# Attention over eight tokens: two head pairs at a time instead of one, with the value products in front of the scores

## The chip, the cores and the metric

One core of a Trainium2 chip runs the whole program. The metric is the device time of one execution in microseconds (us). "TensorE" is PE in the rows (its weight loads are PEld), VectorE is DVE, ScalarE is ACT, GpSimd is POOL, SyncE is SP.

## The reference

Two layers stand behind each other; the change touches only the second. Cut to what matters of it:

```python
xn = _layernorm(x)                                    # x: 8 x 512 x 256
qkv = xn @ W_in.T + b_in                              # read as (s=8, b=512), 16 heads of 64
q = q * 64 ** -0.5
attn = einsum('bhsd,bhtd->bhst', q, k) + einsum('bhsd,std->bhst', q, k_dist)
attn = softmax(attn)                                  # over t = 8 keys
out = einsum('bhst,bhtd->bhsd', attn, v) + einsum('bhst,std->bhsd', attn, v_dist)
s = out @ W_out.T + b_out
g = silu(sqrt((xn @ cos(theta + theta_noise)) ** 2 + (xn @ sin(phi + phi_noise)) ** 2))
x = x + s * g
```

Each of the 512 sequences has only 8 tokens, so a head's scores are 512 little matrices of 8 by 8.

## The kernel before

Layer 1 runs over 8 groups of 512 tokens (64 sequences); the group's number is `i`. Blocks of 32 tokens (4 sequences) are multiplied with themselves, which gives 32 by 32 scores, and `apart` pushes those of other sequences to minus infinity. Every engine has its own program text, and semaphores join them; the order is written out by hand. For TensorE and ScalarE, `layer1_steps` gives it, as a list of steps (kind, k):

- `V`: values of a tile of 128 tokens, half the heads; `Q`, `K`: queries and keys of head pair k (128 rows, 512 tokens); `F`: the gate's two products. Each is six products of 512 columns into one of two PSUM banks `pr`, used in turn; ScalarE reads the bank. `three` (L1598) issues them.
- `S`: the scores of pair k into `s_ps` (L1687), small products on part of the array, into disjoint parts of the banks. The program has 32 of them per pair, and each runs as two, so the profile counts 64.
- `AV`: the value products of pair k into `o_ps` (L1703), again 64 in the profile.
- After the steps, `outputs(t, pairs)` (L1716) multiplies each pair's outputs with `W_out`, three products of 256 columns for each of four tiles t and eight pairs. Tiles 1 and 2 come first, into the `pr` banks. Between them stand the transposes of the next group's tokens (`transposes`, L1607), of the weights summed by distance (L1736), and last the products for these (L1745).

Between S and AV a pair goes through all the other engines: VectorE adds the distance scores (`scores`, L1885) and takes the maximum (L1888), GpSimd subtracts it (L2048), ScalarE takes the exponential (L1771), VectorE sums the keys (`key_sums`, L1896 to L1906), GpSimd multiplies with the reciprocal (`weigh`, L2055), and VectorE transposes (`transposed_blocks`, L1915) into `pt`, which AV reads. ScalarE copies the AV result (L1810, `ot_h`), and VectorE makes its low part (`low_outputs`, L1923), after which `o_ps` is free. `by_distance` (L1943) is 16 instructions of VectorE per group that sum the weights by distance. The intermediates `sc`, `ex`, `pt` have two buffers each, so a pair may follow while the last one is under way.

At the end of a group ScalarE makes the gate (L1815 square root, L1817 tanh, each with a table load) and then reads the next group's transposed tokens (L1760, L1761); VectorE makes their low part (L1851). The transposes share the bank `misc` (`misc_free`), so the one at L1736 must wait until L1851 has read the one before.

Of the kernel before, what the change touches and what calls it, by code (L numbers as in the profile page):

```python
# [19 lines left out]
ALU = mybir.AluOpType  # L20
# [33 lines left out]
HP = H1 // 2  # L54
OT_EARLY = 5
# [102 lines left out]
class Shared:  # L158
# [3 lines left out]
    def __init__(self, nc, ctx):  # L162
# [36 lines left out]
        self.pt = [low[:, i * TOK // 2:(i + 1) * TOK // 2].rearrange("p (h t k) -> p h t k", h=2, t=TT) for i in range(2)]  # L199
# [1213 lines left out]


# [5 lines left out]
def layer1(nc, io, shared, x1_dram, out):  # L1420
    with ExitStack() as ctx:
# [29 lines left out]
        sc, ex = sb("sc", [P, 2, 2, TT, BLK]), sb("ex", [P, 2, 2, TT, BLK])  # L1451
        mx, sm, rc = sb("mx", [P, 2, 2, TT]), sb("sm", [P, 2, 2, TT]), sb("rc", [P, 2, 2, TT])
        ec = sb("ec", [P, 2, 2, TT, NREL])
# [133 lines left out]
        def _(pe):  # L1587
# [55 lines left out]
            def body(i):  # L1643
# [7 lines left out]

                for kind, k in steps:
# [27 lines left out]
                    if kind == "S":  # L1680
                        pe.wait_ge(m.qk_ok, 2 * HP * i + 2 * k + 2)
                        wait(pe, m.sc_ok, HP * i + k)
                        stand_alone(pe, m.pe_passed)
                        for blk in range(NBLK):
                            q, t = blk % 4, blk // 4
                            for h in range(2):
                                mm = pe.matmul(s_ps[BLK * q:BLK * (q + 1), h, BLK * t:BLK * (t + 1)],  # L1687
                                               qt[D1 * h:D1 * (h + 1), k % 2, BLK * blk:BLK * (blk + 1)],
                                               kt[D1 * h:D1 * (h + 1), k % 2, BLK * blk:BLK * (blk + 1)],
                                               start=True, stop=True)  # L1690
                        mm.then_inc(m.s_psum, 1)
                    if kind == "AV":
                        pe.wait_ge(m.pt_ok, HP * i + k + 1)
                        if k == 0:
                            pe.wait_ge(m.v_ok, 2 * TT * (i + 1))
                            wait(pe, m.so_ok, TT * i)
                        wait(pe, m.ot_low, HP * i + k)
                        for blk in range(NBLK):
                            q, t = blk % 4, blk // 4
                            rows = slice(BLK * q, BLK * (q + 1))  # L1700
                            for h in range(2):
                                c = D1 * (2 * k + h)
                                mm = pe.matmul(o_ps[D1 * h:D1 * (h + 1), q, BLK * t:BLK * (t + 1)],  # L1703
                                               v[rows, t, c:c + D1], pt[k % 2][rows, h, t, :], start=True, stop=True)
                        mm.then_inc(m.o_psum, 1)

                def w_bank(t):
                    return (fin, pr[:, through_pr.index(("W", 1)) % 2, :], pr[:, through_pr.index(("W", 2)) % 2, :],
                            o_ps[:, 0, :])[t]

                def outputs(t, pairs):
                    for hp in pairs:
                        tokens = slice(t * P, (t + 1) * P)
# [456 lines left out]
```

## Time and profile before

| | |
|---|---|
| three timed runs | 1199.99, 1203.26, 1204.4 us; median 1203.26 |
| span of the profiled execution | 1204.5 us |
| TensorE, VectorE, ScalarE, GpSimd busy, share of the span | 96%, 75%, 56%, 47% |
| granted TensorE clock, mean over the span | 0.975 |
| layer 1 | about the last 564 us of the span |

The page says how long each engine was busy. A TensorE record lasts longer than the time until the next one starts, because products are pipelined; what a product costs is read from start to start. "Issue" behind an idle time means that the engine waited for nothing that the profile shows.

### The profile page before, as it was taken

The numbers are of one execution on the slowest core, as the hardware profiler recorded it, in microseconds if no ns is written. First come the engines' busy times: TensorE is split into PE (matmuls) and PEld (weight loads), VectorE is DVE, ScalarE is ACT, GpSimd is POOL, SyncE is SP. The second block draws the span as 40 slices with busy tenths as digits, with TensorE's granted clock in tenths as the row PEclk, the third lists the DMA queues.
The fourth block names the chain that finished last, engine by engine and source line by source line (L and its number), as shares of the span: only waits on it lengthen the run. The fifth ranks groups of instructions, "written<-read, shape, count | busy, mean of one in ns | idle before, by whom it ended". The sixth has DMA issues, their size and how long they took to land. (4 is left out here: it accounts for less than half of the span.)

```text
span 1204.5 us, 34940 instructions
## 1 busy us (share of the span) xinstructions
PE 1161.7 (96%) x14327; PEld 755.9 (63%) x14327; DVE 901.2 (75%) x1993; ACT 677.8 (56%) x1302; POOL 571.2 (47%) x599
## 2 busy tenths in 40 slices
PE   6999999999999999999989999999999999999997
PEld 5433444444444444443368787878879787887976
DVE  6777887868788887878275967778687767768766
ACT  4357676776777677666643544445344444535453
POOL 2156686776868586777622413232231413223131
PEclk8589999999999999999989999999999999999999
DMA  8445254553525345352240010010101001010100
GB/s 236 105 96 135 70 138 119 116 151 79 143 71 136 104 115 132 93 156 72 71 127 1 4 54 3 12 46 4 54 4 54 4 16 41 4 54 4 36 4 19
DMA packets 57998, 86.80 MB, mean 72 GB/s; under 512 B 8304, under 2 KB 38256, under 8 KB 57840
## 3 DMA queue, kind: packets, MB, share of 16 engines
q1 hardware_dynamic: 57680, 84.31, 26.6%
q8 instruction: 113, 1.85, 0.6%
q14 instruction: 45, 0.37, 0.1%
q10 hardware_dynamic: 160, 0.26, 0.1%
HBM read 50.40 MB, written 33.55 MB: 70 GB/s over the span
## 5 line engine op out<-in xcount | busy, mean ns | idle before, releaser
L1111 DVE TENSOR_REDUCE negmax<-s_bank 128x1 f32<-128x512 f32 x512 | 330.2, 679 | 74.3 <-PE s_bank L759 73.7
L1306 POOL TENSOR_TENSOR room<-room 128x512 f32<-128x512 f32 x248 | 310.9, 1286 | 121.7 <-ACT room L925 121.7
L925 ACT ACTIVATE room<-t_bank 128x512 f32<-128x512 f32 x512 | 284.1, 600 | 84.2 <-PE t_bank L769 80.6
L769 PE MATMUL t_bank<-qst,kst 50*128 50x512 f32 x512 | 202.6, 472 | 6.1 <-ACT room L925 5.7
L759 PE MATMUL s_bank<-kst,qst 48*128 48x512 f32 x512 | 195.6, 475 | 5.1 <-DVE negmax L1111 2.9
L769 PEld LDWEIGHTS t_bank<-qst,kst 50*128 50x128 f32 x512 | 82.1, 189 | 102.1 <-ACT room L925 62.2
L2068 POOL TENSOR_TENSOR win<-rt,apart 128x512 f32<-128x512 f32 x32 | 41.9, 1331 | 211.6 <-DVE rt L1874 211.6
L1598 PE MATMUL pr<-xt_h,win_h 128*128 128x512 f32 x256 | 105.9, 414 | 0.0
L2055 POOL TENSOR_TENSOR ex<-ex,rc 128x256 f32<-128x256 f32 x64 | 41.7, 652 | 130.1 <-DVE rc L1902 130.1
L1598 PE MATMUL pr<-xt_l,win_h 128*128 128x512 f32 x256 | 100.5, 393 | 0.0
L1598 PE MATMUL pr<-xt_h,win_l 128*128 128x512 f32 x256 | 100.5, 393 | 0.0
L759 PEld LDWEIGHTS s_bank<-kst,qst 48*128 48x128 f32 x512 | 80.7, 195 | 18.4 <-DVE negmax L1111 13.6
L1786 ACT ACTIVATE win<-pr 128x512 f32<-128x512 f32 x64 | 38.4, 601 | 84.2 <-PE pr L1598 84.2
L1794 ACT ACTIVATE qt<-pr,bqkv 128x512 f32<-128x512 f32 x64 | 44.1, 689 | 69.0 <-PE pr L1598 69.0
L1874 DVE SCALAR_TENSOR_TENSOR rt<-r,own,rt 128x256 f32<-128x256 f32 x112 | 69.0, 616 | 4.0
L784 PE MATMUL a_bank<-room,v_even 128*32 128x512 f32 x512 | 69.9, 619 | 0.2
L1943 DVE SCALAR_TENSOR_TENSOR p<-pc,own,p 128x256 f32<-128x256 f32 x128 | 67.1, 524 | 2.8
L784 PE MATMUL a_bank<-room,v 128*32 128x512 f32 x512 | 68.7, 609 | 0.3
L808 PE MATMUL d_bank<-room,pick 128*32 128x512 f32 x496 | 66.2, 606 | 0.0
L1810 ACT ACTIVATE ot_h<-o_ps 128x512 fp32r<-128x512 f32 x64 | 38.3, 599 | 48.0 <-PE o_ps L1703 48.0
L1794 ACT ACTIVATE room<-pr,bqkv 128x512 f32<-128x512 f32 x64 | 44.0, 687 | 29.3 <-PE pr L1598 29.3
L1703 PE MATMUL o_ps<-room,win 32*64 32x32 f32 x4096 | 56.6, 224 | 3.5 <-issue 3.2
(333 smaller groups left out, 2576.2 us busy)
## 6 DMA issues: line engine op xcount, KB each, us to landing
park<-qk_h SPq DMA_DIRECT2D x126, 128.0 KB, 2.4
qst<-park SPq DMA_DIRECT2D x64, 192.0 KB, 3.2
kst<-park SPq DMA_DIRECT2D x64, 192.0 KB, 4.2
park<-qk_l SPq DMA_DIRECT2D x64, 128.0 KB, 2.4
room<-in_x SPq DMA_DIRECT2D x8, 512.0 KB, 5.3
xr<-in_x SPq DMA_DIRECT2D x8, 512.0 KB, 6.0
room<-x SPq DMA_DIRECT2D x8, 512.0 KB, 4.0
out<-so SPq DMA_DIRECT2D x32, 128.0 KB, 1.7
```

The lines of the kernel that those rows point to most:

```text
L759: pe.matmul(s_bank[n % S_BANKS][:, :], qst[slot][rows, j, c * P:(c + 1) * P], kst[slot][rows, j, :], start=True, stop=True).then_inc(m.s_d ...
L769: pe.matmul(t_bank[w % 2][:, :], kst[slot][rows, j, c * P:(c + 1) * P], qst[slot][rows, j, :], start=True, stop=True).then_inc(m.t_done, 1)
L784: mm = pe.matmul(a_bank[BLK * h:BLK * h + BLK, :], v[b % 2][:, c, hg * P + h * DH0:hg * P + (h + 1) * DH0], probs[:, c, h, :], start=(c == ...
L808: mm = pe.matmul(d_bank[BLK * h:BLK * h + BLK, :], pick[:, hf, :], sums[:, pair, h, :], start=first, stop=last)
L925: act.activation(probs[:, c, j, :], t_bank[w % 2][:, :], ACT.Exp, scale=SCALE0).then_inc(m.exp_done, 1)
L1111: dve.tensor_reduce(negmax[:, i_par, 2 * odd + j, c:c + 1], s_bank[n % S_BANKS][:, :], X, ALU.max, negate=True).then_inc(m.max_done, 1)
L1306: add = pool.tensor_tensor(sums[:, pair, h, :], probs[:, 2 * pair, h, :], probs[:, 2 * pair + 1, h, :], ALU.add)
L1598: mm = pe.matmul(dst, a(kc), b(kc), start=(n == 0), stop=(n == 3 * KC - 1))
L1703: mm = pe.matmul(o_ps[D1 * h:D1 * (h + 1), q, BLK * t:BLK * (t + 1)], v[rows, t, c:c + D1], pt[k % 2][rows, h, t, :], start=True, stop=True)
L1794: act.activation((qt, kt)[side][:, k % 2, :], bank, ACT.Identity, bias=bqkv[:, HP * side + k:HP * side + k + 1]).then_inc(m.qk_ok, 1)
L1874: dve.scalar_tensor_tensor(dst, src, own[:, s:s + 1], dst, op0=ALU.mult, op1=ALU.add).then_inc(m.r_sum, 1)
L1943: dve.scalar_tensor_tensor(dst, pc[:, heads, :, :], own[:, s:s + 1], dst, op0=ALU.mult, op1=ALU.add).then_inc(m.p15_sum, 1)
```

## The change

Scores, softmax and value products are done for two head pairs (`PG = 2`, `NG = 4` sets) in one go. A step `S` or `AV` now issues twice as many small products; `sc`, `ex`, `pt`, `mx`, `sm`, `rc`, `ec` hold one set of twice the size and have one buffer instead of two; the instructions on VectorE, GpSimd and ScalarE for a set are one each, of twice the width. `AV` of a set stands directly in front of `S` of the set two later. The last two value steps stand behind all F steps, and between and behind them the output products of tiles 1 and 2 are split by pairs. The semaphore counts follow.

```diff
 def layer1_steps():
-    steps = [("V", k) for k in range(2 * TT)] + [("Q", 0), ("K", 0)]
-    for hp in range(HP):
-        if hp + 1 < HP:
-            steps += [("Q", hp + 1), ("K", hp + 1)]
-        else:
-            steps += [("F", 0)]
-        steps += [("S", hp)]
-        if hp >= 2:
-            steps += [("AV", hp - 2)]
-    return steps + [("F", 1), ("F", 2), ("AV", HP - 2), ("F", 3), ("AV", HP - 1)]
+    def queries_and_keys(g):
+        return [(kind, hp) for hp in range(PG * g, PG * (g + 1)) for kind in "QK"]
+
+    steps = [("V", k) for k in range(2 * TT - 2)] + queries_and_keys(0) + [("V", 2 * TT - 2), ("V", 2 * TT - 1), ("S", 0)]
+    steps += queries_and_keys(1) + [("F", 0), ("S", 1)]
+    for g in range(2, NG):
+        steps += queries_and_keys(g) + [("AV", g - 2), ("S", g)]
+    return steps + [("F", 1), ("F", 2), ("F", 3), ("AV", NG - 2), ("AV", NG - 1)]
+
+EXP_BEFORE = {("Q", 3): 0, ("Q", 5): 1, ("Q", 7): 2, ("F", 3): 3}
...
+                    if (kind, k) == ("AV", NG - 1):
+                        pe.wait_ge(m.wout_low, 1)
+                        pe.wait_ge(m.ot_low, HP * i + PG * (NG - 2))
+                        for t in (1, 2):
+                            free_pr(i, "W", t)
+                            outputs(t, range(PG * (NG - 2)))
                     if kind == "AV":
-                        pe.wait_ge(m.pt_ok, HP * i + k + 1)
+                        pe.wait_ge(m.pt_ok, NG * i + k + 1)
...
-                        wait(pe, m.ot_low, HP * i + k)
+                        wait(pe, m.ot_low, HP * i + PG * k)
...
-                first_pairs, last_pair = range(HP - 1), (HP - 1,)
-                pe.wait_ge(m.wout_low, 1)
-                pe.wait_ge(m.ot_low, HP * i + HP - 1)
-                for t in (1, 2):
-                    free_pr(i, "W", t)
-                    outputs(t, first_pairs)
+                for n, pairs in ((HP - PG, range(PG * (NG - 2), HP - PG)), (HP - 1, (HP - 2,))):
+                    pe.wait_ge(m.ot_low, HP * i + n)
+                    for t in (1, 2):
+                        outputs(t, pairs)
                 pe.wait_ge(m.ot_low, HP * (i + 1))
-                outputs(1, last_pair)
+                outputs(1, (HP - 1,))
                 if not last:
                     transposes(i + 1, 0)
-                outputs(2, last_pair)
+                outputs(2, (HP - 1,))
...
@@ (VectorE, transposed_blocks)
-                wait(dve, m.o_psum, n - 1)
+                wait(dve, m.o_psum, n)
...
@@ (VectorE, the group's body from its second pair set on)
+                for g in range(2, NG):
+                    scores(i, g)
+                    for j in range(PG):
+                        low_outputs(i, PG * (g - 2) + j)
+                    key_sums(i, g)
+                    by_distance(i, 0, range(4 * (g - 2), 4 * (g - 2) + 2))
+                    transposed_blocks(i, g)
+                    if g < NG - 1:
+                        by_distance(i, 0, range(4 * (g - 2) + 2, 4 * (g - 1)))
+                for j in range(PG):
+                    low_outputs(i, HP - 2 * PG + j)
+                by_distance(i, 0, range(NREL - 2, NREL))
+                by_distance(i, 1, range(2))
+                for j in range(PG):
+                    low_outputs(i, HP - PG + j)
+                by_distance(i, 1, range(2, NREL))
```

On TensorE, in the middle of a group, the program before has this at a value step (`s_ps` are scores, `o_ps` value products, `pr` the last rows of K and the first of the next Q):

```order
L1598 MATMUL pr<-xt_h,win_l_66 128x512
L1687 MATMUL s_ps<-room,qt 32x32 x32
L1703 MATMUL o_ps<-room,win 64x32 x32
L1598 MATMUL pr<-xt_h,win_h_63 128x512
L1598 MATMUL pr<-xt_l,win_h_63 128x512
```

It comes six times in a group, with 12 products of 512 columns between two of them. Now the same place reads

```order
L1596 MATMUL pr<-xt_h,win_l_66 128x512
L1722 MATMUL o_ps<-room,win 64x32 x64
L1698 MATMUL s_ps<-room,qt 32x32 x64
```

It comes twice in a group, with 24 products of 512 columns ahead of it: 128 small products of the program stand in one run where 64 stood. The other value and score steps stand alone now, 64 in a run.

On VectorE, from the last transpose of weights to the group's end, the program before has (`p` is `by_distance`, `ot_l` the low part of a pair's outputs, `xt_l` that of the next group's tokens)

```order
L1915 STREAM_TRANSPOSE room<-ex 128x256
L1923 TENSOR_TENSOR ot_l_late<-o_ps,ot_h_49 128x512
L1943 SCALAR_TENSOR_TENSOR p<-pc,own,p 128x32x8 x3
L1923 TENSOR_TENSOR ot_l_late<-o_ps,ot_h_49 128x512
L1943 SCALAR_TENSOR_TENSOR p<-pc,own,p 128x32x8 x5
L1950 COPY pd<-p 128x16x4
L1951 TENSOR_TENSOR pd<-p 128x16x4x7
L1851 TENSOR_TENSOR xt_l<-o_ps,xt_h 128x512
```

and now

```order
L1917 STREAM_TRANSPOSE room<-ex 128x512
L1925 TENSOR_TENSOR ot_l_50<-o_ps,ot_h_49 128x512
L1925 TENSOR_TENSOR ot_l_late<-o_ps,ot_h_49 128x512
L1945 SCALAR_TENSOR_TENSOR p<-pc,own,p 128x32x8 x4
L1925 TENSOR_TENSOR ot_l_late<-o_ps,ot_h_49 128x512 x2
L1945 SCALAR_TENSOR_TENSOR p<-pc,own,p 128x32x8 x6
L1952 COPY pd<-p 128x16x4
L1953 TENSOR_TENSOR pd<-p 128x16x4x7
```

Two low parts (pairs 4 and 5) and ten sums by distance stand behind the last transpose now, where one low part and eight sums stood between the last transpose and the last low part's end.

## Rows read from the trace of the kernel before

**Rows 1.** The page: busy time of two engines; the queue of instruction blocks
```profile
PE 1161.7 (96%) x14327; PEld 755.9 (63%) x14327; DVE 901.2 (75%) x1993; ACT 677.8 (56%) x1302; POOL 571.2 (47%) x599
...
q8 instruction: 113, 1.85, 0.6%
```

**Rows 2.** Windows: two groups of layer 1 (window, us, busy us of each engine, clock)
```profile
920.16:989.70 69.54, 69.12 (x1326) 58.12 (x1325) 52.68 (x127) 33.13 (x53) 20.32 (x27) 1.00 0.08 25
989.70:1060.83 71.13, 69.30 (x1325) 58.20 (x1325) 52.73 (x127) 32.99 (x53) 20.30 (x27) 1.00 0.08 25
```

**Rows 3.** Waits of TensorE's products, 640 to 1204 us (us, times, longest)
```profile
PE o_ps L1703 <- issue: 3.2, 5, 0.9
PE pr L1598 <- issue: 1.2, 1, 1.2
PE s_ps L1687 <- issue: 0.6, 2, 0.4
PE o_ps L1703 <- DVE ot_l_late L1923: 0.2, 1, 0.2
```

**Rows 4.** Timeline of TensorE, 881 to 884 us (start, length, engine, line, tiles)
```profile
881.27 0.39 PE L1598 MATMUL pr<-xt_l,win_h 128*128 128x512 f32 x1
881.50 0.40 PE L1598 MATMUL pr<-xt_h,win_l 128*128 128x512 f32 x1
881.82 0.76 PE L1687 MATMUL s_ps<-room,qt 64*32 64x32 f32 x64
882.51 0.86 PE L1703 MATMUL o_ps<-room,win 32*64 32x32 f32 x64
883.30 0.50 PE L1598 MATMUL pr<-xt_h,win_h 128*128 128x512 f32 x1
883.64 0.39 PE L1598 MATMUL pr<-xt_l,win_h 128*128 128x512 f32 x1
```

**Rows 5.** Timeline of TensorE, 1031 to 1038 us
```profile
1031.44 0.76 PE L1687 MATMUL s_ps<-room,qt 64*32 64x32 f32 x64
1032.13 0.86 PE L1703 MATMUL o_ps<-room,win 32*64 32x32 f32 x64
1034.17 0.50 PE L1598 MATMUL pr<-cs_h,xt_h 128*128 128x512 f32 x1 [1.18 <-issue]
...
1035.77 0.76 PE L1687 MATMUL s_ps<-room,qt 64*32 64x32 f32 x64
1036.45 0.79 PE L1703 MATMUL o_ps<-room,win 32*64 32x32 f32 x57
1037.89 0.31 PE L1703 MATMUL o_ps<-room,win 32*64 32x32 f32 x7 [0.65 <-issue]
```

**Rows 6.** DMA, 1030 to 1040 us: what was moved in 40 slices of 0.25 us
```profile
GB/s 0 0 0 0 0 0 0 66 0 0 0 0 0 0 0 0 0 0 0 0 0 0 66 0 0 0 0 0 0 0 0 0 0 0 33 0 0 0 0 0
```

**Rows 7.** Timeline of TensorE, 895 to 896 us
```profile
895.44 0.66 PE L1703 MATMUL o_ps<-room,win 32*64 32x32 f32 x40
```

**Rows 8.** Groups by form, 860 to 930 us (count, busy us, mean ns, idle before)
```profile
L1943 DVE SCALAR_TENSOR_TENSOR p<-pc,own,p 128x256 f32<-128x256 f32 x16 | 8.2, 514 | 0.4
```

**Rows 9.** Timeline of ScalarE, 903 to 911 us
```profile
903.69 0.60 ACT L1810 ACTIVATE ot_h<-o_ps 128x512 fp32r<-128x512 f32 x1 [0.29 <-PE o_ps L1703]
...
907.98 1.06 ACT L1817 ACTIVATE room<-room 128x1024 f32<-128x1024 f32 x1
909.71 0.60 ACT L1760 ACTIVATE room<-o_ps 128x512 f32<-128x512 f32 x1 [0.67 <-PE o_ps L1607]
910.20 0.59 ACT L1761 ACTIVATE xt_h<-o_ps 128x512 fp32r<-128x512 f32 x1
```

**Rows 10.** Timeline of TensorE, 909 to 913 us
```profile
909.08 0.60 PE L1607 MATMUL o_ps<-ident,room 128*128 128x128 f32 x4
...
912.75 0.60 PE L1736 MATMUL o_ps<-ident,pd 128*128 128x128 f32 x4
```

**Rows 11.** Timeline of VectorE, 902 to 911 us
```profile
910.83 0.69 DVE L1851 TENSOR_TENSOR xt_l<-o_ps,xt_h 128x512 fp32r<-128x512 f32 x1 [2.47 <-ACT xt_h L1761]
```

More of the change, by code:

```diff
@@ L1650, in body, with w_bank, outputs @@
                 pe.wait_ge(m.xt_low, KC * (i + 1))
+                def w_bank(t):
+                    return (fin, pr[:, through_pr.index(("W", 1)) % 2, :], pr[:, through_pr.index(("W", 2)) % 2, :],
+                            o_ps[:, 0, :])[t]
+                def outputs(t, pairs):
+                    for hp in pairs:
+                        tokens = slice(t * P, (t + 1) * P)
+                        for n, (x, w) in enumerate(((ot_h[:, hp, tokens], wout_h), (ot_h[:, hp, tokens], wout_l),
+                                                    (ot_l(hp)[:, tokens], wout_h))):
+                            pe.matmul(w_bank(t)[:, 0:E], x, w[:, hp, :], start=(hp == 0 and n == 0), stop=False)
                 for kind, k in steps:
@@ L1705, in body @@
-                        mm.then_inc(m.o_psum, 1)
[L1707 to L1713, printed above, removed]
-                        for n, (x, w) in enumerate(((ot_h[:, hp, tokens], wout_h), (ot_h[:, hp, tokens], wout_l),
-                                                    (ot_l(hp)[:, tokens], wout_h))):
-                            pe.matmul(w_bank(t)[:, 0:E], x, w[:, hp, :], start=(hp == 0 and n == 0), stop=False)
@@ L1718, in body @@
-                first_pairs, last_pair = range(HP - 1), (HP - 1,)
-                pe.wait_ge(m.wout_low, 1)
-                pe.wait_ge(m.ot_low, HP * i + HP - 1)
-                for t in (1, 2):
-                    free_pr(i, "W", t)
-                    outputs(t, first_pairs)
+                        wait(pe, m.ot_low, HP * i + PG * k)
+                        for j in range(PG):
+                            for blk in range(NBLK):
+                                q, t = blk % 4, blk // 4
+                                rows = slice(BLK * q, BLK * (q + 1))
+                                at = TT * BLK * j + BLK * t
+                                for h in range(2):
+                                    c = D1 * (2 * (PG * k + j) + h)
+                                    mm = pe.matmul(o_ps[D1 * h:D1 * (h + 1), q, at:at + BLK],
+                                                   v[rows, t, c:c + D1], pt[rows, 2 * j + h, t, :], start=True, stop=True)
@@ L2075, in body @@
                 pool.memset(p15[:, :, :, :], 0.0).then_inc(m.p15_zero, 1)
-                for k in range(HP):
-                    if k >= 1:
-                        weigh(i, k - 1)
-                    less_maximum(i, k)
-                    if k == 2 and not last:
-                        rstd_of(i + 1)
-                for t in range(TT):
-                    if t == TT // 2:
-                        weigh(i, HP - 1)
-                    pool.wait_ge(m.sq_ok, TT * i + t + 1)
-                    if t == 0:
-                        wait(pool, m.x2_ok, TT * i)
-                    pool.tensor_tensor(q2[:, t, :], sq[:, t % 2, 0:E], sq[:, t % 2, E:2 * E], ALU.add).then_inc(m.q2_ok, 1)
+                less_maximum(i, 0)
+                weigh(i, 0)
+                squares_sum(i, 0)
+                less_maximum(i, 1)
+                if not last:
+                    rstd_of(i + 1)
+                weigh(i, 1)
+                less_maximum(i, 2)
+                weigh(i, 2)
+                less_maximum(i, 3)
+                squares_sum(i, 1)
+                squares_sum(i, 2)
+                weigh(i, 3)
+                squares_sum(i, 3)
             over_batches(body)
```

173 lines of the change are left out of this document (81 added, 92 removed).

## The prediction, made before the changed kernel had run

> **What bounds the kernel now.** I read the page first. TensorE is busy 96% of the span, VectorE 75% [rows 1], so what counts is what TensorE issues and where it stops. Then the windows: a group of layer 1 takes 69.5 us, another 71.1 us, at the full clock, with the same products and nearly the same busy time of every engine [rows 2]. The reader is to see that 1.6 us went without any engine working more. Third, the waits of TensorE's products in layer 1: VectorE held them up for 0.2 us in all 564 us, nobody else did, but 5.0 us in eight waits is "issue" [rows 3]. So no data is late anywhere, and VectorE's load is not the bound: whatever the change takes from it lies beside TensorE's work and is costed at nothing.
>
> Fourth, the timeline, from start to start. A product of 512 columns takes 0.23 us. The last one in front of small products takes 0.32 (881.50 to 881.82), the first one behind them 0.34 (883.30 to 883.64). 64 score products take 0.69 us, 64 value products 0.79 [rows 4]. Fifth, the "issue" waits. Scores of one pair and its value products, from 1031.44 on, should be over after 0.69 + 0.79 = 1.48 us; the next product starts only at 1034.17, 2.73 us after them. The next such stop comes after 6 + 64 + 57 = 127 products, at 1037.89 [rows 5]. A product is two instructions, the weight load and the product, so the first stretch holds 128 times 2 = 256 instructions, and the second 254 and a few waits. The page has a queue "instruction" with 113 transfers and 1.85 MB, 16 KB each, for 2 times 14327 = 28654 instructions and some waits: about 256 in a block [rows 1]. In the slices one such block is moved at 1031.75 to 1032.0 and the next at 1035.5 to 1035.75 [rows 6]: each starts after TensorE has entered a block and is needed at that block's end. So TensorE stops wherever it runs through 256 instructions faster than the next block comes. With large products 256 instructions last many us; only small ones are fast enough.
>
> **The change, part by part.** (1) Fewer passages and longer runs. A group had ten runs of small products (S0, S1, six of S and AV, AV6, AV7) and has six. A passage in and out costs 0.32 + 0.34 - 2 x 0.23 = 0.20 us, so four fewer give 0.8 us. Within a run, the small products that come later are the cheaper ones: 40 of them make a record of 0.66 us [rows 7], 64 one of 0.86 [rows 4], so 24 cost 0.20 us, 8.3 ns each, where the step's mean is 11 or 12. 64 more in a step then cost 0.53 instead of 0.69 or 0.79. Two pairs cost 0.69 + 0.79 + 2 x 0.53 = 2.54 us against 2.96, four times in a group 1.7 us. Together 2.5 us in each of 8 groups: -20 us. No row shows a step of 128. Bounds: if the second 64 cost as much as the first, only the passages are left, -6 us; at the 7.6 ns between the records of 40 and of 57 (0.66 and 0.79 us) [rows 5, 7] it is -22. I take -20, because the second half of a step already runs as the additional products would.
>
> (2) Whole blocks of small products. A run of 512 instructions (AV and S, 128 products of the program, 256 in the profile) always holds at least one whole block of 256, wherever the blocks' limits fall. There are two such runs in a group, 16 in all. The work of such a block is 128 x 8.3 ns = 1.1 us and some 0.1 at the step's change, 1.2. What a block takes at least, when it begins with small products, is 2.73 us in one row and 3.72 in the other [rows 5], so 1.5 to 2.5 us are lost each time. The 2.73 belongs to a block that begins right behind large products, where the sequencer has run ahead and asks early; the new blocks mostly begin in the middle of small ones. I take 2.2: 16 x 2.2 = +35 us, bounds +24 and +40. Of the stops of before, 5.0 us of idle time and about 0.2 more each that the length of the records hides, 7 us, I let 6 go [rows 3]: runs of 256 instructions remain, but a stop in them needs the block's limit close to the run's start.
>
> The Trainium skill has this in "Runtime: NRT & Kernel Launch", section "Instruction fetch mechanics": an engine's instructions come in blocks of 16 KiB, 256 of them, the next asked for while one runs. The trace agrees, with 16 KB in each of 113 transfers. The same section gives TensorE room for 2048 instructions and says that the fetch is mostly hidden; by that a run of 512 would cost nothing, and the sum would end below before. A box beside it speaks of two lines of 16 KiB only, and by that the stops come; the stop at 1034.17 speaks for the box.
>
> (3) The group's end. ScalarE copies the last values, makes the gate and then reads the next tokens' transposes; VectorE takes their low part; only then is the bank free for the transposes at L1736. Before, ScalarE's copy starts at 903.69 and ends at 904.29, the gate behind it lasts until 909.04, 4.75 us, and the two reads end at 910.79 [rows 9], VectorE at 911.52 [rows 11], and TensorE wants the bank at 912.75 [rows 10]: 1.2 us to spare. TensorE fills the time from 903.6 with 72 products of 256 columns and a transpose; 45 of them up to 909.08 make 0.122 us each. Now 24 of the 72 stand ahead of the last value step. Behind it are 48: 5.9 us, 0.4 for the transposes and 0.2 for passages, 6.4. ScalarE has two copies there, 1.1 us (the spacing of its reads is 0.5), then 4.75 + 1.08, and VectorE 0.7: 7.7 us with a hand-over. TensorE waits 1.3 us in seven groups, +9. Ahead of it the last value step must wait until VectorE has taken the low parts of pairs 4 and 5, which stand behind the last weights' transpose and the sums by distance at 0.51 us each [rows 8]; I reckon 0 to 0.8 us late, 0.25 taken, +2. The wait for pair 6's low part, behind four more such sums (2.1 us), mostly lies inside the 1.3. Together +11, bounds +6 and +18. Queued behind these waits on TensorE is all the rest of the group, so they count in full.
>
> Sum: -20 + 35 - 6 + 11 = +20 us, on the profiled 1204.5: 1224.5. The median of the runs shown is 1.2 lower, so 1223 for the timed run. The step from large to small products has no other wait in it: the drain of K by ScalarE (0.7 us) lies under the 1.3 us of value products in front of the scores. Without that cover it would cost about 0.7 us twice a group, 11 us.
>
> **The rivals.** (a) The blocks cost nothing: if instructions are held further ahead than I think, and the stops in the rows have another reason, +35 falls away and the old stops stay. Then -20 + 11 = -9, between -16 and +1: 1194, on the other side. For it speaks that only eight stops stand in 48 runs of 256 instructions; against it that two stops lie 256 instructions apart to within a few, with a transfer between. It decides at a block's price of 2.1 us: with less than 0.9 lost in each of 16, the other terms (-20 - 6 + 11) are larger. (b) A cheap block, 1.3 us lost as at 1034.17: +21 instead of 35, 1209. The sequencer would have to run ahead in the small products too. (c) One buffer for `sc`, `ex`, `pt`: the last set's chain through four engines must be done in the 18 F products, 64 values and 24 outputs, 4.1 + 1.3 + 2.9 = 8.3 us. The wider instructions bring it near 8 us. If it is 1 to 2 us late in each group, +8 to +16: 1235. (d) The change does as little as the passages (-6 us in part 1), all else as forecast: 1237.
>
> **How the numbers follow.** A measurement tells about 0.5%, 6 us, from no change: 1197 to 1209. Chances: forecast (1213 to 1231) 0.50; (a) 0.16, in the lower half faster by over 0.5%; (b) 0.16 (1204 to 1213); (c) and (d) together 0.18 (1231 to 1246). The range 1203 to 1241 leaves out (a), and little of (c) and (d). Faster 0.12, within 0.5% 0.12, slower 0.76. Of the cases that are slower, the forecast's own range is 1213 to 1231.
>
> **What would show it.** The profile after must have one "issue" stop in each AV and S run, 16 of them, of 1.5 to 2.5 us, with the products between whole stops a multiple of 128; two blocks moved within 4 us around it; 128 scores alone in 1.2 us and 128 values in 1.3; at L1736 a wait of about 1.3 us for VectorE's L1855; no wait at S for ScalarE. I am wrong if the runs of 256 products go through in 2.6 us, if a block comes sooner in the middle of small products than behind large ones, or if TensorE's waits for VectorE's transposes grow beyond 1 us a group.

## The result, and the profile after

The kernel after takes 1260.51 us (median of 4 runs, 1254.01 to 1264.69), the kernel before 1203.83 beside it (4 runs, 1199.99 to 1206.49). The ratio is 1.0468, 95% interval 1.0432 to 1.0504: 57 us slower, where I had forecast 20, and above the upper end of my range (1241). The profiled span is 1258.0 us against 1204.5.

The page of the kernel after, against [rows 1]: busy time of the engines, the granted clock in 40 slices, the queue of instruction blocks.

```profile
PE 1165.2 (93%) x14327; PEld 768.3 (61%) x14327; DVE 893.1 (71%) x1769; ACT 669.6 (53%) x1270; POOL 561.9 (45%) x535
...
PEclk9699999999999999999899998988999999999988
...
q8 instruction: 113, 1.85, 0.6%
```

TensorE has the same products and is busy only 3.5 us longer; its share fell from 96% to 93%. VectorE has fewer instructions and less busy time than before, which bought nothing. There are 113 blocks of instructions, as before. The row PEclk has five eights from its 25th slice on (755 us), where that of before has nines only: there the clock was granted at half for a while.

The waits of TensorE's products in layer 1 (us, times, longest), against [rows 3]; L1722 are value products, L1698 scores, L1659 output products, L1742 the transposes of the summed weights:

```profile
PE s_ps L1698 <- issue: 27.1, 15, 2.4
PE o_ps L1722 <- issue: 8.5, 5, 2.3
PE o_ps L1722 <- DVE ot_l_late L1925: 8.1, 6, 1.6
PE o_ps L1742 <- DVE xt_l L1855: 3.4, 5, 0.8
PE pr L1659 <- DVE ot_l_late L1925: 3.0, 5, 1.9
PE pr L1659 <- issue: 1.6, 1, 1.6
```

"Issue" has grown from 5.0 us in 8 waits to 37.2 in 21. Counted from start to start less the usual spacing, and with stops of 0.3 us and more, it is 6.8 us in 9 before and 43.2 in 22 now. Beside it stand waits for VectorE at three places, 14.5 us, where 0.2 was. One of these, the longest at L1659 (1.9 us, 855.16 us), I count among the stops: it too stands where a block of instructions begins. In fact each of these stops, the 9 of before and the 22 of now, begins at the same place when TensorE's instructions (weight loads, products, semaphore waits) are counted off in blocks of 256, to within two instructions.

The timeline of TensorE at one AV and S run, with the clock's fall behind it (start, length, tiles):

```profile
977.42 1.49 PE L1722 MATMUL o_ps<-room,win 32*64 32x32 f32 x128
978.84 0.99 PE L1698 MATMUL s_ps<-room,qt 64*32 64x32 f32 x93
982.07 0.46 PE L1698 MATMUL s_ps<-room,qt 64*32 64x32 f32 x35 [2.24 <-issue]
982.46 0.67 PE L1596 MATMUL pr<-xt_h,win_h 128*128 128x512 f32 x1
982.93 0.63 PE L1596 MATMUL pr<-xt_l,win_h 128*128 128x512 f32 x1
983.36 0.63 PE L1596 MATMUL pr<-xt_h,win_l 128*128 128x512 f32 x1
...
986.44 0.40 PE L1596 MATMUL pr<-xt_l,win_h 128*128 128x512 f32 x1
```

The run of 256 products stops behind the 221st for 2.4 us. Then the products of 512 columns start every 0.43 us, not every 0.23 as in [rows 4], until 986. What was moved in those 10 us (975 to 985, 40 slices of 0.25 us):

```profile
GB/s 0 0 0 0 0 0 0 0 0 0 0 0 0 0 0 0 66 0 0 0 0 0 0 0 0 0 0 0 0 0 0 0 66 0 0 0 0 0 0 0
```

The transfer of the block that begins with the last 35 products starts in the slice at 979.0, some 0.8 us after the block before it was entered (128 products before the stop, about 978.3), and its first product comes at 982.07. The second transfer is the next block's, at 983.0, 1 us after this one was entered.

Windows of the same trace (window, us, busy us of each engine, clock, DMA, GB/s): a whole group, a quiet stretch, and the stretch behind the stop.

```profile
870.88:945.55 74.67, 69.33 (x1326) 59.01 (x1325) 51.86 (x99) 31.98 (x49) 19.20 (x19) 0.98 0.08 24
955.00:975.00 20.00, 20.00 (x332) 16.24 (x331) 11.71 (x24) 8.74 (x14) 9.69 (x11) 1.00 0.01 3
...
982.60:986.00 3.40, 3.40 (x9) 2.63 (x10) 2.57 (x4) 0.69 (x1) 1.05 (x1) 0.50 0.02 5
```

The group takes 74.7 us where [rows 2] had 69.5 and 71.1, with the same products. Behind the stop the granted clock is 0.50, that is 1.2 GHz for 2.4. While TensorE worked on layer 1 there were 14 such stretches, each 3.4 or 6.8 us long, and before there was none. In all of them together the products of the whole array took 21 us more than their usual spacing, and with the small products it is 24. (In the experiments below the half clock is counted on the products of the whole array alone.)

The ledger of layer 1, all counted from start to start in the two profiled executions:

| us | forecast | measured |
|---|---|---|
| passages, longer runs | -20 | -17 |
| stops in the 16 AV and S runs | +35 | +30 (13 long ones of 1.8 to 2.6, mean 2.2; two of 0.6 and 0.7) |
| stops elsewhere, less those of before | -6 | +6 (13.1 in 7, less 6.8) |
| waits for VectorE at the group's end | +11 | +15 (8.5 ahead of the last value step, 6 behind it) |
| half clock | nothing | +24 |
| sum | +20 | +57 (before rounding; layer 1 is 57 longer) |

### The profile page after: what moved, and what is told of

Its sections match the earlier page's. It is cut to its first block, busy times and chain, and to the rows that moved or that the text cites. A ratio compares the mean times of both kernels' runs of the same rounds, so it can differ in the third digit from the quotient of the medians.

```text
span 1258.0 us, 34401 instructions
## 1 busy us (share of the span) xinstructions
PE 1165.2 (93%) x14327; PEld 768.3 (61%) x14327; DVE 893.1 (71%) x1769; ACT 669.6 (53%) x1270; POOL 561.9 (45%) x535
## 4 chain that ended last, share of the span: by engine, by line
PE 40%; issue 5%; DVE 3%; ACT 3%; POOL 0%; DMA 0%; ACTq 0%; DVEq 0%; SPq 0%
PE pr L1596 25%; PE s_ps L1698 3%; PE o_ps L1722 3%; PE o_ps L1659 3%; PE pr L1659 2%; PE o_ps L1636 1%; DVE p L1945 1%; PE pr L1751 1%; DVE ec L1899 1%; ACT L1819 1%; PE pr L1622 0%; PE o_ps L1751 0%; ACT room L1821 0%; ACT room L1819 0%; PE o_ps L1742 0%
## 5 line engine op out<-in xcount | busy, mean ns | idle before, releaser
L770 PE MATMUL t_bank<-qst,kst 50*128 50x512 f32 x512 | 199.0, 464 | 7.3 <-ACT room L926 5.8
L760 PE MATMUL s_bank<-kst,qst 48*128 48x512 f32 x512 | 191.7, 465 | 5.3 <-DVE negmax L1112 2.9
L1596 PE MATMUL pr<-xt_l,win_h 128*128 128x512 f32 x256 | 103.7, 405 | 0.0
L1899 DVE TENSOR_REDUCE ec<-ex 128x128 f32<-128x512 f32 x32 | 35.7, 1115 | 69.6 <-ACT ex L1777 69.6
L2056 POOL TENSOR_TENSOR sc<-sc,mx 128x512 f32<-128x512 f32 x32 | 33.7, 1052 | 107.3 <-DVE mx L1892 107.3
L1945 DVE SCALAR_TENSOR_TENSOR p<-pc,own,p 128x256 f32<-128x256 f32 x128 | 77.0, 601 | 3.7
L2063 POOL TENSOR_TENSOR ex<-ex,rc 128x512 f32<-128x512 f32 x32 | 36.9, 1154 | 92.7 <-DVE rc L1905 92.7
L1698 PE MATMUL s_ps<-room,qt 64*32 64x32 f32 x4096 | 44.7, 202 | 27.1 <-issue 27.1
L1814 ACT ACTIVATE ot_h<-o_ps 128x512 fp32r<-128x512 f32 x64 | 34.8, 595 | 65.5 <-PE o_ps L1722 65.5
```

The source lines that it names most:

```text
L760: pe.matmul(s_bank[n % S_BANKS][:, :], qst[slot][rows, j, c * P:(c + 1) * P], kst[slot][rows, j, :], start=True, stop=True).then_inc(m.s_d ...
L770: pe.matmul(t_bank[w % 2][:, :], kst[slot][rows, j, c * P:(c + 1) * P], qst[slot][rows, j, :], start=True, stop=True).then_inc(m.t_done, 1)
L1596: mm = pe.matmul(dst, a(kc), b(kc), start=(n == 0), stop=(n == 3 * KC - 1))
L1698: mm = pe.matmul(s_ps[BLK * q:BLK * (q + 1), h, c:c + BLK], qt[D1 * h:D1 * (h + 1), j, BLK * blk:BLK * (blk + 1)], kt[D1 * h:D1 * (h + 1), ...
L1945: dve.scalar_tensor_tensor(dst, pc[:, heads, :, :], own[:, s:s + 1], dst, op0=ALU.mult, op1=ALU.add).then_inc(m.p15_sum, 1)
```

## The experiments

My theory after the result had two parts. First, TensorE stops where its instructions come to an end sooner than the next block, and this costs 36 us. Second, behind such a standstill the clock is granted at half for a while, some 24 us, whatever the standstill came from. The rivals: the stops belong to the order AV in front of S, or to a bank, and not to the length of the run; the half clock has another cause, such as the kind or number of small products; or what counts is the one-buffered chain through the other engines.

**Shorter runs, AV and S apart (e1).** On the kernel after; each AV step two steps earlier:

```diff
-        steps += queries_and_keys(g) + [("AV", g - 2), ("S", g)]
+        steps += queries_and_keys(g)[:2] + [("AV", g - 2)] + queries_and_keys(g)[2:] + [("S", g)]
```

> The changed kernel, with each AV moved from in front of S to between the two head pairs' Q and K, so that no run of small products is longer than 256 instructions. Theory (the length of a run sets the stops, and a stop of about 2 us or more makes the granted clock fall): the 15 or so stops of about 2.3 us inside AV and S runs go (some 31 us), most of the half-clock stretches behind them too (about 14 us), two passages a group come back (+3 us): about 1219 us, between 1212 and 1228. Rival (the doubled width of the softmax with one buffer is what costs, and TensorE would stop elsewhere as long): 1248 us or more, with waits for VectorE or ScalarE in place of the issue stops.

Measured: 1270.29 us (1269.78 to 1270.99), ratio 1.0528 [1.0502, 1.0554]. A miss, by more than 40 us, and a time in the rival's range. Its waits:

```profile
PE s_ps L1698 <- ACT room L1802: 13.9, 16, 0.9
PE s_ps L1698 <- issue: 12.0, 6, 2.4
...
PE o_ps L1722 <- issue: 5.8, 6, 2.5
PE o_ps L1722 <- DVE ot_l L1925: 5.2, 8, 0.9
```

Waits for ScalarE and VectorE have come, as the rival said, and the issue stops have stayed, as it did not. Apart, the scores stand right behind K and wait for ScalarE's drain, 16 times 0.9 us: the cover that the prediction priced at 11 us when lost. The value step waits for VectorE. And the stops did not go: from start to start 16 of them, 26.9 us, though no run is longer than 128 products. So "a run of 128 is free" was wrong; with the half clock (17.7 us) nothing was won.

**VectorE's low parts first (e2).** On the kernel after; in the last set, the low parts of pairs 4 and 5 ahead of the transpose instead of two sums by distance, which go behind it:

```diff
                     key_sums(i, g)
-                    by_distance(i, 0, range(4 * (g - 2), 4 * (g - 2) + 2))
+                    if g < NG - 1:
+                        by_distance(i, 0, range(0, 2))
+                    else:
+                        for j in range(PG):
+                            low_outputs(i, HP - 2 * PG + j)
                     transposed_blocks(i, g)
...
```

> The changed kernel, with VectorE's low parts of pairs 4 and 5 ahead of the last transpose of weights, in the place of two sums by distance, which go behind it. Theory (the last value step waits 1.4 us in each group for these low parts): that wait goes, 11 us, and some 3 to 5 us of half clock behind it: 1244 to 1250 us. Rival (the wait moves on to the end of the group, to pair 6's low part or to the transposes at the weights by distance): 1254 to 1262 us.

Measured: 1250.48 us (1246.29 to 1252.6), ratio 1.0359 [1.0326, 1.0391]: 10 us better than after, and half a us above the theory's 1244 to 1250. Each against the kernel before that ran beside it, it is 43.5 us for 56.7, 13 us better. The wait ahead of the last value step is gone; stops (21, 36.4 us) and half clock (20.7 us) are what they were. So 10 to 13 of the 57 us were the order on VectorE, and the rest was not.

What made VectorE late is in its timeline in the kernel after:

```profile
990.32 1.79 DVE L1945 SCALAR_TENSOR_TENSOR p<-pc,own,p 128x256 f32<-128x256 f32 x2
...
992.66 0.96 DVE L1945 SCALAR_TENSOR_TENSOR p<-pc,own,p 128x256 f32<-128x256 f32 x2
...
1000.92 2.15 DVE L1945 SCALAR_TENSOR_TENSOR p<-pc,own,p 128x256 f32<-128x256 f32 x2
1003.00 0.70 DVE L1917 STREAM_TRANSPOSE room<-ex 128x512 f32<-128x512 f32 x1
1003.62 0.64 DVE L1925 TENSOR_TENSOR ot_l<-o_ps,ot_h 128x512 fp32r<-128x512 f32 x1
1004.20 0.67 DVE L1925 TENSOR_TENSOR ot_l_late<-o_ps,ot_h 128x512 fp32r<-128x512 f32 x1
```

and in that of GpSimd:

```profile
1000.75 1.16 POOL L2063 TENSOR_TENSOR ex<-ex,rc 128x512 f32<-128x512 f32 x1 [1.48 <-DVE rc L1905]
1001.87 0.92 POOL L2071 TENSOR_TENSOR room<-room 128x256 f32<-128x256 f32 x1
```

Two sums by distance take 0.96 us alone, as in [rows 8], and 2.15 beside two instructions of GpSimd, 1.79 beside one. The transpose must follow them, the low parts must follow it, and TensorE, ready at 1003.5, gets its value step at 1005.01. The transpose is over at 1003.70, so the weights themselves are late by 0.2 us at most; the rest is the low parts.

**The same extra products, spread (e3) or bunched (e4).** On the kernel before. Both kernels issue 256 extra small products per group (repeats of ones already there). The first doubles four steps, so that four more runs in a group have 128 products in the profile; the second makes one value step five times as long:

```diff
-                        for blk in range(NBLK):
+                        for blk in [n % NBLK for n in range(NBLK * (2 if k < 2 else 1))]:
...
-                        for blk in range(NBLK):
+                        for blk in [n % NBLK for n in range(NBLK * (2 if k >= HP - 2 else 1))]:
```

> The kernel before, with the small products of S0, S1, AV6 and AV7 issued twice (the second time they write the same values again): 4 times 64 products more in a group, each in a run of at most 256 instructions. Both theories: 4 x 0.53 us in each of 8 groups, 17 us, and at most 5 us of stops where a block's limit falls close to a run's start: 1218 to 1227 us.

```diff
-                        for blk in range(NBLK):
+                        for blk in [n % NBLK for n in range(NBLK * (5 if k == 2 else 1))]:
```

> The kernel before, with the small products of AV2 issued five times in a row: the same number of products more as in the kernel that spreads them, but one run of 768 instructions in each group. Nothing in the softmax is wider. Theory (run length): 2 or 3 whole blocks in each run, 16 to 24 stops of 2.3 to 2.5 us and half-clock stretches behind them: 17 + 45 + 15, about 1280 us, between 1255 and 1295. Rival (instructions come fast enough; the width of the softmax or its single buffers are the cause): the same as with the products spread, within 5 us.

Measured: spread 1245.49 us (1237.14 to 1248.31), ratio 1.0304 [1.0252, 1.0355]; bunched 1271.32 (1269.86 to 1273.6), ratio 1.0537 [1.0508, 1.0567]. With the same number of small products, bunching costs 26 us more. The timeline of the bunched kernel, with the whole blocks of its value step:

```profile
825.98 1.49 PE L1703 MATMUL o_ps<-room,win 32*64 32x32 f32 x128
829.55 1.48 PE L1703 MATMUL o_ps<-room,win 32*64 32x32 f32 x128 [2.08 <-issue]
833.28 1.17 PE L1703 MATMUL o_ps<-room,win 32*64 32x32 f32 x64 [2.25 <-issue]
834.38 0.79 PE L1598 MATMUL pr<-xt_h,win_h 128*128 128x512 f32 x1
834.97 0.63 PE L1598 MATMUL pr<-xt_l,win_h 128*128 128x512 f32 x1
```

There are exactly 128 products, 256 instructions, between two stops, and 3.7 us from the one to the other, of which 1.3 are work. No AV in front of S, no single buffer, no change on another engine is in this kernel: the length of the run does it. From start to start it has 20 stops of 36.0 us and 13.7 us of half clock, the spread one 19 of 18.2 and 7.8. With the small products the half clock is 20 against 9 us, and the difference in stops and half clock, 29 us, is that of the two lengths of layer 1, 28. (The whole spans differ by 23.4: layer 0, which no edit touches, took 5 us longer in the spread kernel's profiled execution.) The spread kernel missed the 1218 to 1227 that I expected for both theories, because, again, runs of 128 products stopped too.

**Only the end of the group (e5).** On the kernel before: the last two value steps behind all F steps, and the first half of the output products of tiles 1 and 2 between them.

```diff
-    return steps + [("F", 1), ("F", 2), ("AV", HP - 2), ("F", 3), ("AV", HP - 1)]
+    return steps + [("F", 1), ("F", 2), ("F", 3), ("AV", HP - 2), ("AV", HP - 1)]
...
+                    if (kind, k) == ("AV", HP - 1):
+                        pe.wait_ge(m.wout_low, 1)
+                        pe.wait_ge(m.ot_low, HP * i + HP - 4)
+                        for t in (1, 2):
+                            free_pr(i, "W", t)
+                            outputs(t, range(HP - 4))
```

> The kernel before, one head pair at a time, with the end of a group alone as in the changed kernel: all F steps ahead of the last two value steps, the outputs of four pairs on tiles 1 and 2 between these two. Theory (the group's end costs by itself, because 24 products less stand behind the last value step while ScalarE makes the gate): a wait of about 1 us at L1736 for the next tokens' low part in seven groups, 7 us, no wait ahead of the last value step, since one pair's chain is short: 1210 to 1218 us. Rival (the end costs only because the chain of the doubled set is late): 1200 to 1208 us.

Measured: 1207.78 us (1205.12 to 1209.42), ratio 1.0044 [1.0027, 1.0062], less than the theory's 1210 to 1218 and just inside the rival's 1200 to 1208. Its wait at the transposes of the summed weights:

```profile
PE o_ps L1740 <- DVE xt_l L1855: 5.9, 7, 0.8
```

So this wait, which I had forecast at 1.3 us in seven groups, is real and 0.8 to 1.0 long, 7.1 us in all from start to start. Layer 1 is only 3.7 us longer, as the stops are 3.5 us in this execution and were 6.8. The group's end by itself costs 5 us of the 57.

**Half sets in the middle (e6).** On the kernel with low parts first: each middle AV and S step in two halves, with three Q, K or F steps between (`AV0`, `S0` are the first pair of a set, no semaphore at their end).

```diff
-    for g in range(2, NG):
-        steps += queries_and_keys(g) + [("AV", g - 2), ("S", g)]
-    return steps + [("F", 1), ("F", 2), ("F", 3), ("AV", NG - 2), ("AV", NG - 1)]
+    steps += [("Q", 4), ("K", 4), ("Q", 5), ("AV0", 0), ("S0", 2), ("K", 5), ("Q", 6), ("AV", 0), ("S", 2),
+              ("K", 6), ("Q", 7), ("AV0", 1), ("S0", 3), ("K", 7), ("F", 1), ("AV", 1), ("S", 3)]
+    return steps + [("F", 2), ("F", 3), ("AV", NG - 2), ("AV", NG - 1)]
...
```

> The changed kernel with the low parts first as in the run before, softmax of two pairs in one go and single buffers kept, but in the middle of a group TensorE issues each AV and S in two halves of 64 products, apart from each other by large products, so that no run is longer than 256 instructions and the K in front of each S is drained. Theory (run length): of the stops in AV and S runs almost nothing stays, nor of the half clock behind them; against the run with the low parts first (1250) 30 us of stops and 12 us of half clock less, 5 us of passages more: about 1213, between 1204 and 1222. Rival (the doubled width and single buffers cost in the middle of the group): 1235 or more, with waits for VectorE or ScalarE there.

**Whole sets, AV and S apart and covered (e7).** On the same: AV behind a Q, S behind the next Q, so that K's drain lies under products.

```diff
-    for g in range(2, NG):
-        steps += queries_and_keys(g) + [("AV", g - 2), ("S", g)]
-    return steps + [("F", 1), ("F", 2), ("F", 3), ("AV", NG - 2), ("AV", NG - 1)]
+    steps += [("Q", 4), ("K", 4), ("Q", 5), ("AV", 0), ("K", 5), ("Q", 6), ("S", 2), ("K", 6), ("Q", 7), ("AV", 1),
+              ("K", 7), ("F", 1), ("S", 3)]
+    return steps + [("F", 2), ("F", 3), ("AV", NG - 2), ("AV", NG - 1)]
```

> As the kernel in halves, but whole steps of 128 products, each AV and each S apart from the other by 12 large products, and a Q or an F between the last K and its S. Theory (a stop needs a whole block of small products, or a sequencer that stands at a wait as it enters a block and so asks late for the next): no stops in the middle of a group except a few under 1 us, and fewer passages than in halves: 1208, between 1198 and 1220. Rival (two steps of 256 instructions with only 24 between them are still too fast for the blocks): 1225 to 1240 with stops of about 1 us at every second step.

Measured: halves 1231.92 us (1226.32 to 1234.51), ratio 1.0241 [1.0206, 1.0277]; covered 1234.47 (1231.74 to 1236.54), ratio 1.0267 [1.0238, 1.0297]. Both missed the theory's range (1204 to 1222, 1198 to 1220) upwards; the covered one lies in its rival's (1225 to 1240), the halves between theory and rival. In the halves kernel the stops are down to 10 of 12.5 us and the half clock to 5.6, but new waits for VectorE have come, 20 us in 29. In the covered one the waits of e1 are gone, and the stops are not: 17, of 30.9 us. One of them in its timeline:

```profile
743.56 0.24 PE L1722 MATMUL o_ps<-room,win 32*64 32x32 f32 x2 [0.56 <-issue]
743.73 0.51 PE L1596 MATMUL pr<-xt_h,win_h 128*128 128x512 f32 x1
...
746.70 1.17 PE L1698 MATMUL s_ps<-room,qt 64*32 64x32 f32 x114
749.69 0.29 PE L1698 MATMUL s_ps<-room,qt 64*32 64x32 f32 x14 [1.81 <-issue]
```

and what was moved from 740 to 755 us (40 slices of 0.375):

```profile
GB/s 0 0 0 44 0 0 0 0 0 0 0 0 0 0 0 0 0 0 0 44 0 0 0 0 0 0 0 0 0 0 0 0 0 0 0 0 44 0 0 0
```

A block is entered at 743.56, behind a short stop: 2 small products, 12 large ones, 114 small ones, 128 in all. It has 3 us of large products in it, ample time for a transfer. But the transfer of the next block starts only in the slice at 747.1, 3.6 us or more after this one was entered, where in the kernel after it was 0.8 and 1 us. The stop follows, and behind it the next transfer, at 753.5, is 3.8 us late again. In the traces a transfer this late comes where a block was entered behind a stop or a wait and had fewer than about 62 instructions of small products left ahead of its large ones; with more left it was never seen. But not every such block is late: in the kernel after, one with 16 such instructions left, entered at 749.37 behind a stop of 2.3 us, had its next transfer 1.1 us later. The pattern may explain why runs of 128 products stopped in e1, e3 and this kernel, and how one stop brings the next. No run changed it alone, so it is not shown as a cause.

In one group no block limit fell badly, and it is the best of any trace here:

```profile
938.82:1008.01 69.19, 67.73 (x1328) 57.43 (x1326) 51.43 (x99) 32.10 (x49) 18.86 (x19) 1.00 0.08 25
```

Even so it is only 0.35 us shorter than the good group of [rows 2]: there was little to win in pairing the head pairs in this order.

**The order turned (e8).** On the kernel after, S in front of AV:

```diff
-        steps += queries_and_keys(g) + [("AV", g - 2), ("S", g)]
+        steps += queries_and_keys(g) + [("S", g), ("AV", g - 2)]
```

> The changed kernel with S in front of AV, as the order was before the change. The stops stay, since a run has the same 512 instructions; S now waits for ScalarE to drain the last K, which AV covered: about 0.9 us in each of 16 runs, 14 us, perhaps more where that wait makes the sequencer ask late for a block: 1270 to 1285 us. Rival (the order of the two does not matter, since the run is held up by blocks anyway, and the wait lies under that): 1256 to 1264 us.

Measured: 1298.87 us (1293.5 to 1306.22), ratio 1.0815 [1.076, 1.087]; more than the 1270 to 1285 expected. Two of its waits:

```profile
PE o_ps L1722 <- issue: 38.8, 20, 2.5
PE s_ps L1698 <- ACT room L1802: 13.9, 16, 0.9
```

The stops stay (25 of 47.5 us from start to start) and stand at the value products now, since these are second: they belong to the run, not to a bank or an order. K's drain by ScalarE is bare, 13.9 us. The half clock grew by 15.6 us, to 36.7, which nothing in the edit explains but more standing still. That is what the next two are for.

**A wait instead of a stop (e9, e10).** On the kernel before, with its own products and blocks: one wait in each group, long, or two, short.

```diff
+                    if (kind, k) == ("AV", 3):
+                        pe.wait_ge(m.sub_ok, HP * i + k + 3)
```

> The kernel before, where TensorE waits once in a group, ahead of AV3, for GpSimd's subtraction of pair 5: a standstill of about 2.0 us that has nothing to do with blocks of instructions. Theory (a standstill of more than about 1.6 us makes the granted clock fall to half for 3.4 or 6.8 us, whatever its reason): 16 us of waiting and 1.5 to 3 us of half clock behind most of the eight, 8 to 20 us: 1228 to 1240 us. Rival (the clock falls from something else in the long runs, as from the small products' low load): the waiting alone, 1217 to 1222 us, with no half-clock stretch in layer 1.

```diff
+                    if kind == "AV" and k in (1, 3):
+                        pe.wait_ge(m.mx_ok, HP * i + k + 3)
```

> The kernel before, where TensorE waits twice in a group, ahead of AV1 and AV3, for VectorE's maximum of the pair two later: 16 standstills of about 1.25 us, 20 us together, more than the eight long ones. Theory: no half-clock stretch, since each is short, so about 1222 to 1227 us, less than with the one long wait in a group. Rival (idle time in sum is what counts for the clock): half-clock stretches here too, 1232 us or more.

Measured: one wait 1223.49 us (1217.41 to 1233.89), ratio 1.0144 [1.0099, 1.0189]; two waits 1223.02 (1221.2 to 1223.78), ratio 1.0155 [1.0129, 1.018]. The first kernel: one of the waits in TensorE's timeline, and its sum.

```profile
753.88 0.76 PE L1687 MATMUL s_ps<-room,qt 64*32 64x32 f32 x64
756.60 1.18 PE L1705 MATMUL o_ps<-room,win 32*64 32x32 f32 x64 [1.96 <-POOL sc L2050]
...
758.73 0.63 PE L1598 MATMUL pr<-xt_h,win_l 128*128 128x512 f32 x1
759.15 0.63 PE L1598 MATMUL pr<-xt_h,win_h 128*128 128x512 f32 x1
```

```profile
PE o_ps L1705 <- POOL sc L2050: 15.7, 8, 2.0
```

The second kernel, the same two views:

```profile
747.04 0.76 PE L1687 MATMUL s_ps<-room,qt 64*32 64x32 f32 x64
749.06 0.86 PE L1705 MATMUL o_ps<-room,win 32*64 32x32 f32 x64 [1.27 <-DVE mx L1890]
...
750.42 0.39 PE L1598 MATMUL pr<-xt_h,win_l 128*128 128x512 f32 x1
```

```profile
PE o_ps L1705 <- DVE mx L1890: 19.8, 16, 1.3
```

From the last score to the next value it is 2.15 us in the first kernel and 1.40 to 1.47 in the second. Behind 6 of the 8 long waits the clock fell to half for 3.4 or 6.8 us (10.9 us lost in this execution); behind the 16 short ones it fell once (1.3 us lost), though they stand still longer in sum. The small products are those of before, and no late block stands just ahead of a fall: a standstill in one piece is enough. The rival, that the fall needs a late block or longer runs of small products, is out. Whether it needs small products beside it stays open: every standstill of this length here has them on one side at least. The times are less sharp than the traces. The kernel with one wait missed its 1228 to 1240, and two of its four runs lie in the rival's 1217 to 1222; its trace is that of its slowest run. The medians are equal, as 16 us of standstill and its clock happen to cost what 20 us without it do, and the one-wait kernel scatters over 16 us: its four runs have a mean clock of 0.979, 0.978, 0.970 and 0.962 at 1217, 1220, 1227 and 1234 us. How often the fall comes differs from run to run.

**A shorter bunch (e11).** On the kernel before, one value step three times as long:

```diff
+                        for blk in [n % NBLK for n in range(NBLK * (3 if k == 2 else 1))]:
```

> The kernel before, with the small products of AV2 three times in a row: one run of 512 instructions in each group, as the changed kernel has two of. 128 products more, 1.06 us, 8.5 us in all. Theory: one stop of 2.2 to 2.5 us in each of the eight, 19 us, and half clock behind most of them, 8 to 16 us: 1238 to 1250 us. Rival (a run of 512 costs nothing by itself): 1210 to 1214 us.

Measured: 1237.34 us (1233.75 to 1238.84), ratio 1.0271 [1.0241, 1.0302], just under the theory's 1238 to 1250 and far from the 1210 to 1214 of a kernel without stops. 128 extra products a group are 9 us of work in all; the other 24 are stops (20.9 us from start to start, 6.8 before) and half clock (10.1). It is a run of the length that the change has, alone, in a kernel that has nothing else of the change.

## Why the prediction was wrong

The step that failed is one that the sum does not have: it put the clock at nothing, and the half clock behind the new standstills cost 24 us. Its direction and its main mechanism were right: the eight "issue" waits of [rows 3] and the pair of [rows 5] do show blocks of 256 instructions that come late, and runs of 512 meet more of them. Rival (a), blocks that cost nothing, and (b), cheap ones, are out by e4 and e11. Rival (c), a late chain of the last set, foresaw a wait that came, ahead of the last value step and of the size it gave (8.5 us), but not its reason: in e2, with the low parts ahead of the transpose, nothing of that wait is left, so the chain with its single buffers was on time. By its steps:

(1) **Passages and longer runs, -20.** Measured -17. 128 scores alone take 1.22 us, as forecast; 128 values 1.42 and not 1.32; both together 2.65 and not 2.54. Small miss, from the price of the second 64.

(2) **Whole blocks, 16 times 2.2.** The size of a stop was right (mean 2.2), with some luck: the 3.72 us that I gave to a block of small products in [rows 5] belong to one with six large products at its head. The bunched kernel's 3.7 are of small ones alone. The number of the stops was 13 of 16. In three runs the whole block began 17 to 19 products into the run, and the transfer of the next one had started 0.6 to 0.9 us before it was entered. That is no rule: with the order turned (e8) blocks that began as near to the run's start had it 0.9 to 1.1 us after. Two of the three show no stop at all, as here:

```profile
902.75 1.49 PE L1722 MATMUL o_ps<-room,win 32*64 32x32 f32 x128
904.16 1.30 PE L1698 MATMUL s_ps<-room,qt 64*32 64x32 f32 x128
```

So "at least one whole block" is true and does not yet mean a stop. The term gave 30 us. What failed is the half sentence that of the stops of before "I let 6 go". Stops outside these runs did not go; they are 7, of 13.1 us, six of them of 1.6 us and more in the two value steps at the group's end or right behind one. In three of them (697.07, 1081.83 and 1237.52) the block before had been entered behind a stop or a wait, and the transfer started 2.8 to 4.1 us after that. In the other three a block began with the value step or one product ahead of it, so that its 128 products were a whole block of their own. The term as a whole came to +36 instead of +29.

(3) **The group's end, +11.** Measured 15. The wait at the transposes is 1.0 us from start to start, forecast 1.3. But the last value step waits 1.2 to 1.7 us in six of the eight groups, not 0.25: I had taken a sum by distance at the 0.51 us of [rows 8], a mean of places where GpSimd was mostly idle, and now two of them stand beside GpSimd's `weigh`, which starts on the same reciprocal as they do, and take twice as long. e2 puts them behind, and wins 10 us. (Of the eight sums that stood behind the last transpose before, three, and not all eight, were ahead of the last low part.)

(4) **The clock, which no step speaks of.** This is the largest error, 24 us, and alone it is more than the way to the upper end of the range. I had read the granted clock of 1.00 in both groups of [rows 2] and taken it as given. But no stop of before is longer than 1.25 us beyond the usual spacing, and the change's stops of 2.2 us were a length that [rows 3] did not have. Each of the 14 falls in layer 1 after comes with or just behind a standstill of 1.6 us or more (here from one product's start to the next), 12 of them one of 1.8 or more. Eight more such standstills, five of them of 1.8 or more, brought none. The Trainium skill, "TensorE: Matmul & The Clock Gate", section "Part 1: The HAM clock gate (the "warmup" mystery)", says that an engine that has been idle is clocked at 1.2 GHz and returns to 2.4 once it has been busy for a while. The rows agree with both levels and with the return (products every 0.43 us, then every 0.23 again), and by the page's rule I should have asked of each standstill that I added whether it brings a fall. That a standstill is enough, without a late block, is what e9 against e10 shows, in one trace of each.

Open: how much of each timed run the clock takes, since only one execution per kernel has a trace; why some standstills of 2.3 to 2.4 us are followed by no fall (those that began at 671.04, 694.72, 991.77 and 1131.98 in the kernel after); at which instruction exactly a block is asked for; and the late ask, which is a pattern and was not tested alone. No version ran faster than the kernel before; the nearest, the changed end alone, is 0.4% slower.

## What to carry to other kernels

When instructions become smaller or stand closer together, count them in blocks: how many us of work is one block of TensorE's instructions, against the 3 to 4 us that a block took here when the engine ran dry. A bound engine's standstills have two prices, their length and the clock behind them, and the second is invisible in a profile in which all standstills are short. And wider instructions on engines with time to spare saved nothing here; look rather at what a shared start with another engine does to the duration of the few that something waits for.

## What the runs showed of the hardware

- A block of 256 instructions of small products is 1.1 to 1.3 us of work, and took 3.6 to 3.7 us in the bunched kernel (829.55 to 833.28). All 22 stops of the kernel after stand where a block of 256 begins.
- A block entered behind a stop may, but need not, have the next one's transfer start 3.6 us after its entry instead of 1 (743.56 and 747.1 us in the covered kernel).
- Behind standstills of 2.15 us the granted clock fell to half in 6 of 8, behind those of 1.4 to 1.47 us in 1 of 16 (e9, e10); a product of 512 columns then takes 0.43 us instead of 0.23. Once, in the kernel with three times one value step, a standstill of 1.14 us was followed by a fall; four of 2.3 to 2.4 us in the kernel after were followed by none.
- Two scalar-tensor-tensor instructions of VectorE took 0.96 us alone and 2.15 beside tensor-tensor instructions of GpSimd on other data.
